# Two graph attention layers on one core: both layers as one program over one arena, the second layer's first loads issued during the last head of the first

## The chip, the cores and the metric

The kernel runs on one core of a Trainium2 chip. The core has five engines with instruction streams of their own: TensorE (matmul), VectorE, ScalarE (ACT), GpSimd (POOL) and SyncE (SP), which here issues all DMA transfers. They meet only through semaphores. The metric is the device time of one execution in microseconds; lower is better.

## The reference

N = 4096 nodes with 256 features, an adjacency matrix of 4096 x 4096 integers. Two layers of masked attention, each followed by a residual addition and a layer norm:

```python
def _gat(x, adj, W_heads, a1, a2, W_out, b_out):            # layer 0: 8 heads of 128
    Wh = jnp.einsum('nf,hfd->hnd', x, W_heads)
    s1 = jnp.einsum('hnd,hd->hn', Wh, a1)
    s2 = jnp.einsum('hnd,hd->hn', Wh, a2)
    e = s1[:, :, None] + s2[:, None, :]
    e = jnp.where(e > 0, e, ALPHA * e)                      # ALPHA = 0.2
    e = jnp.where(adj[None, :, :] > 0, e, NEG)              # NEG = -9e15
    att = jax.nn.softmax(e, axis=-1)
    hp = jax.nn.elu(jnp.einsum('hnm,hmd->hnd', att, Wh))
    feat = jnp.transpose(hp, (1, 0, 2)).reshape(N, NHEADS * NHID)
    return feat @ W_out + b_out
...
x = _layernorm(x + _L0_gnn_ref(x, adj, ...), axis=-1)
x = _layernorm(x + _L1_gnn_ref(x, L1_gnn_W, L1_gnn_a, adj), axis=-1)   # 4 heads of 64, same masked attention, no elu
```

## The kernel before, in words

The attention weights are never computed one by one. With e = s1 + s2, the exponential of the leaky ReLU is one of two products: exp(s1) exp(s2) where e > 0, and the same with the slope 0.2 elsewhere. So for each head and each block of rows the kernel makes two 0/1 patterns (e > 0, and not, each masked by the adjacency) in fp8 and multiplies them with scaled copies of the head's projected features ("u" and "v", each as a high and a low fp16 part), with a column for the sum of the weights.

**Layer 0** (`first_layer`) packs the adjacency into bytes, projects x for all heads, and then runs 64 groups, g = 0 to 63: head g // 8, row block g % 8 of 512 rows. A group is a sweep over 8 column chunks. For each chunk ACT compares (L512), VectorE splits the result into the two patterns (L655, L656), and TensorE multiplies (L426, 256 matmuls in a group) into four output tiles of 128 rows. After the last chunk ACT and VectorE take the sums from PSUM (L530, L661), VectorE divides (`divide`, L669 to L687), ACT takes the exponential for the elu (L518), VectorE adds it (`add_exponentials`, L691), and SP stores the block to the tensor feat in HBM (`store`, L293). The exponential and the addition of group g - 1 come after the first pattern of group g; for group 63 nothing follows. GpSimd makes the next head's operands (`make`) while TensorE sweeps this head; head 7's are its last work in this layer. The pattern buffers are four deep.

**Layer 1** (`second_layer`) begins with a projection stage of 32 row tiles t: load a tile of feat (`load_feat`, 128 rows, all 1024 columns), turn it with 8 transposes (L964), copy it out of PSUM in two halves (ACT L1071, VectorE L1190), multiply by W_out (L974), add x and bias, normalise (`normalise`, L1199 to L1208, with a square root on ACT, L1086), turn the result (L983), compute its scores (L989, L992). VectorE's `weights` (L1216, L1217) makes the columns that the scores multiply by. Then come the operands of 4 heads and 16 sweeps over 1024 rows each (L1023).

The order is written out by hand in each engine's stream; there is no scheduler. Each layer is a block: all five engines meet at its end (L114) and branch into the next. Layer 0 ends when SP has seen its last store land (`sp.wait_ge(s_st, 16 * G)`), and each layer allocates its own buffers. Layer 1's weights are therefore loaded at the start of its block, and TensorE's stream there begins with:

```python
            turn(0)
            pe.wait_ge(s_w, 96)
            for t in range(NT):
                if t + 1 < NT:
                    turn(t + 1)
                if t == 2:
                    pe.wait_ge(s_wa, 1)
                if t > 1:
                    scores(t - 2)
                project(t)
                if t > 0:
                    turn_x1(t - 1)
```

## Time and profile before

| | |
|---|---|
| median of 3 runs | 2853.63 us (2853.56 to 2857.46) |
| the profiled execution | 2853.23 us, its span 2851.1 us |
| TensorE matmuls busy | 2715.6 us, 95% of the span |
| weight loads | 2350.4 us, 82% |
| ACT | 2049.5 us, 72% |
| VectorE | 1964.6 us, 69% |
| GpSimd | 571.5 us, 20% |

The page of the profile cuts the span into 40 slices and gives each engine's busy share in tenths. The lines of TensorE, of its clock and of the DMA engines:

```profile
PE   7889999999999999999999999999979959999997
PEclk9999999999999999999999999999989989999999
DMA  7985521101010100110111111000054253233330
```

Layer 0 fills the first 29 slices, the projection stage of layer 1 the next three, the operands of its heads the 33rd, its sweeps the rest. TensorE is full in nearly all of them; less full are the start, the passage between the layers, the operand stage, and the end.

### The profile page before, as it was taken

The numbers are of one execution on the slowest core, as the hardware profiler recorded it, in microseconds if no ns is written. First come the engines' busy times: TensorE is split into PE (matmuls) and PEld (weight loads), VectorE is DVE, ScalarE is ACT, GpSimd is POOL, SyncE is SP. The second block draws the span as 40 slices with busy tenths as digits, with TensorE's granted clock in tenths as the row PEclk, the third lists the DMA queues.
The fourth block names the chain that finished last, engine by engine and source line by source line (L and its number), as shares of the span: only waits on it lengthen the run. The fifth ranks groups of instructions, "written<-read, shape, count | busy, mean of one in ns | idle before, by whom it ended". The sixth has DMA issues, their size and how long they took to land. (4 is left out here: it accounts for less than half of the span.)

```text
span 2851.1 us, 62563 instructions
## 1 busy us (share of the span) xinstructions
PE 2715.6 (95%) x26702; PEld 2350.4 (82%) x26702; DVE 1964.6 (69%) x3079; ACT 2049.5 (72%) x3213; POOL 571.5 (20%) x447
## 2 busy tenths in 40 slices
PE   7889999999999999999999999999979959999997
PEld 3448887888888888888888888888868849999997
DVE  5456678777677776776776777755544468889887
ACT  4457876878787878777777777777612279999996
POOL 0130026323232322321432323300011150000000
PEclk9999999999999999999999999999989989999999
DMA  7985521101010100110111111000054253233330
GB/s 257 398 302 174 168 88 40 34 25 40 22 36 19 42 28 26 36 33 25 37 29 30 36 30 29 23 21 23 13 168 143 95 188 105 86 106 106 110 110 16
DMA packets 189144, 235.19 MB, mean 82 GB/s; under 512 B 13594, under 2 KB 113050, under 8 KB 188860
## 3 DMA queue, kind: packets, MB, share of 16 engines
q1 hardware_dynamic: 188868, 231.20, 25.2%
q8 instruction: 211, 3.46, 0.5%
q14 instruction: 65, 0.53, 0.1%
HBM read 180.49 MB, written 50.66 MB: 81 GB/s over the span
## 5 line engine op out<-in xcount | busy, mean ns | idle before, releaser
L426 PE MATMUL l_ps<-l_uv,l_bc 128*128 128x258 f16 x16384 | 1835.1, 273 | 7.2 <-POOL l_uv L246 3.4
L426 PEld LDWEIGHTS l_ps<-l_uv,l_bc 128*128 128x128 fp8e4 x16384 | 1592.4, 97 | 247.7 <-DVE l_bc L656 4.8
L512 ACT ACTIVATE l_bc<-l_s1b,l_kc 128x512 fp8e4<-128x512 f32 x2048 | 1281.3, 708 | 89.3 <-PE l_ps L426 89.2
L655 DVE SCALAR_TENSOR_TENSOR l_bc<-l_bc,mask_t 128x512 uint32<-128x512 uint32 x512 | 468.3, 915 | 410.4 <-ACT l_bc L512 408.0
L1023 PE MATMUL l_ps<-l_uv,l_bc 128*128 128x130 f16 x8192 | 489.2, 221 | 44.7 <-DVE l_bc L1297 41.2
L1023 PEld LDWEIGHTS l_ps<-l_uv,l_bc 128*128 128x128 fp8e4 x8192 | 484.2, 98 | 49.9 <-DVE l_bc L1297 48.4
L656 DVE TENSOR_TENSOR l_bc<-l_bc,mask_t 128x512 uint32<-128x512 uint32 x512 | 489.1, 955 | 0.0
L1116 ACT ACTIVATE l_bc<-l_s1b,l_kc 128x1024 fp8e4<-128x1024 f32 x432 | 453.5, 1140 | 0.7 <-PE l_ps L1023 0.5
L239 POOL TENSOR_TENSOR l_tu<-l_whx,l_eu 128x516 f32<-128x516 f32 x56 | 63.7, 1138 | 1172.9 <-PE l_ps L426 1171.1
L530 ACT COPY l_e<-l_ps 128x258 f32<-128x258 f32 x256 | 93.5, 368 | 245.2 <-PE l_ps L426 245.2
L661 DVE SCALAR_TENSOR_TENSOR l_e<-l_ps,l_sc,l_e 128x258 f32<-128x258 f32 x256 | 116.8, 480 | 148.0 <-ACT l_e L530 148.0
L1296 DVE SCALAR_TENSOR_TENSOR l_bc<-l_bc,mask_t 128x1024 uint32<-128x1024 uint32 x128 | 157.1, 1227 | 32.3 <-ACT l_bc L1116 30.9
L1297 DVE TENSOR_TENSOR l_bc<-l_bc,mask_t 128x1024 uint32<-128x1024 uint32 x128 | 156.6, 1224 | 0.0
L393 PE MATMUL l_ps<-mask_t 128*128 128x512 f32 x264 | 129.0, 628 | 0.0
L974 PE MATMUL l_ps<-l_uv 128*128 128x256 f32 x512 | 119.4, 386 | 0.3 <-issue 0.3
L518 ACT ACTIVATE l_e<-l_e 128x512 f32<-128x512 f32 x64 | 40.6, 635 | 109.7 <-DVE l_e L687 109.7
L239 POOL TENSOR_TENSOR l_tv<-l_whx,l_ev 128x516 f32<-128x516 f32 x64 | 93.0, 1453 | 89.4 <-DMA l_whx<-l_wh 88.5
L974 PEld LDWEIGHTS l_ps<-l_uv 128*128 128x128 f32 x512 | 95.2, 191 | 18.7 <-issue 7.0
L246 POOL TENSOR_TENSOR l_uv<-l_tv,l_uv 128x516 f16<-128x516 f32 x64 | 97.1, 1518 | 28.0 <-DVE l_uv L642 28.0
L240 POOL TENSOR_TENSOR l_uv<-l_whx,l_ev 128x516 f16<-128x516 f32 x64 | 93.3, 1458 | 0.0
L617 DVE TENSOR_SCALAR l_uv<-l_uv 128x1024 fp8e4<-128x1024 int32 x52 | 40.3, 775 | 74.3 <-ACT l_uv L496 74.3
L1082 ACT COPY l_bc<-l_ps 128x256 f32<-128x256 f32 x32 | 11.9, 372 | 107.6 <-PE l_ps L983 107.6
(156 smaller groups left out, 1461.8 us busy)
## 6 DMA issues: line engine op xcount, KB each, us to landing
l_uv<-in_adj SPq DMA_DIRECT2D x128, 512.0 KB, 7.1
l_uv<-uv SPq DMA_DIRECT2D x128, 260.0 KB, 5.2
l_s1b<-l_srow SPq DMA_DIRECT2D x64, 256.0 KB, 3.3
l_whx<-l_wh SPq DMA_DIRECT2D x64, 256.0 KB, 4.5
feat<-l_e SPq DMA_DIRECT2D x64, 256.0 KB, 2.4
l_uv<-feat SPq DMA_DIRECT2D x32, 512.0 KB, 3.8
l_wh<-l_bc SPq DMA_DIRECT2D x38, 256.0 KB, 9.2
uv<-l_uv SPq DMA_DIRECT2D x8, 1040.0 KB, 4.7
```

The costliest lines, as they stand in the source:

```text
L239: nc.gpsimd.tensor_tensor(t[:, :, :], whx[k][:, :, :], factor(f, h, c), ALU.mult)
L393: last = nc.tensor.matmul(banks[i % 3], rowsof, wall[:, k, q * H // 2:(q + 1) * H // 2, :], start=(k == 0), stop=(k == KF - 1))
L426: last = nc.tensor.matmul(sums(t, m), pattern(k, m).bitcast(F8)[:, j, t * P:(t + 1) * P], uv[:, slot(h, order[k]) + j, 2 * m * W1:2 * (m + ...
L512: ins = act.activation(pattern(k, 0).bitcast(F8)[:, j, :], s1b[q][:, :], ACT.Relu, bias=kc[:, h, jt:jt + 1], scale=STEEP, saturate=False)
L655: dve.scalar_tensor_tensor(c, v, ONE8X4, m, ALU.bitwise_xor, ALU.bitwise_and)
L656: dve.tensor_tensor(v, v, m, ALU.bitwise_and).then_inc(s_bc, 1)
L661: dve.scalar_tensor_tensor(e1[:, t, :], sums(t, 1), sc[:, g // NB, at:at + 1], e1[:, t, :], ALU.mult, ALU.add).then_inc(s_ev, 1)
L974: last = nc.tensor.matmul(py[t % 2], ft[t % 2][:, k, :], wo[:, k, :], start=(k == 0), stop=(k == KO - 1))
L1023: last = nc.tensor.matmul(sums(t, m), pattern(k, m).bitcast(F8)[:, j, t * P:(t + 1) * P], uv[:, q, at:at + 2 * W1], start=(k == 0 and j == ...
L1116: ins = act.activation(pattern(k, 0).bitcast(F8)[:, j, :], s1b[:, q, :], ACT.Relu, bias=kc[:, g % H, jt:jt + 1], scale=STEEP, saturate=False)
L1296: dve.scalar_tensor_tensor(c, v, ONE8X4, m, ALU.bitwise_xor, ALU.bitwise_and)
L1297: dve.tensor_tensor(v, v, m, ALU.bitwise_and).then_inc(s_bc, 1)
```

## The change

One function, `network`, and one block take the place of the two. The buffers of both layers are views of one array, `arena`, at byte offsets written out by hand; layer 1's views overlap those of layer 0, and semaphores order the reuse. The identity matrix, which lay in a buffer that layer 0 later overwrites, gets a tensor of its own, and layer 1 uses the same one.

- SP: `load_next` issues layer 1's weights and the first four tiles of x in group 57 (g == LAST + 1), after waiting for head 7's operands and for the end of head 6's sweeps. Feature tiles 0 to 2 are issued in group 60, tile 3 in group 63 after three chunks. `load_feat` waits for the store of the row block that it reads. The store of group 63 is issued in the projection stage at t = 1.
- TensorE: the transposes of feature tiles 0 and 1 follow the last sweep; waits for single evacuations protect the PSUM banks.
- VectorE: `weights` is cut in two and runs inside groups 60 and 61; its reduction for the largest weight moves to t = 4. The division of group 63 comes after the copies of feature tiles 0 and 1, its addition after the normalisation of tile 0.
- ACT: the exponential of group 63 comes after the copies of tiles 0 and 1. The activation at the start of layer 1 that loaded the square root's table is gone.
- GpSimd: adds the bias to the first four x tiles when they land.

The diff, cut to its core (functions of layer 1 that are only renamed, with a 2 at their end, are left out):

```diff
-def first_layer(nc, mask_t, x, adj, W, a1, a2, feat):
+def network(nc, x, adj, W, a1, a2, feat, W_out, b_out, Wn, c1, c2, x1, out):
...
+        mask_t = s.sb("mask", [P, NT, N], U8)
+        arena = s.sb("arena", [P, 96208], U8)
+        ident_t = s.sb("ident", [P, P], F32)
+        ident = ident_t[:, :]
...
+        uv = at(0, F16, 2, (CPB + TWIN) * JC, 4 * W1)
+        bc = at(53664, U8, 1, nbuf, 2, JC * blk)
...
+        z = at(75168, F32, 4, TPB2, F)
+        e2 = at(83360, F32, 4, TPB2, 2 * V1)
+        wall2 = at(87552, F32, 4, KF2, HD2 + 2 * H2)
...
+        wo = low_half[:, 0:2 * K].rearrange("p (k f) -> p k f", k=KO)
+        fin = [low_half[:, (2 + u) * K:(3 + u) * K] for u in range(4)]
+        ft = [low_half[:, (6 + p) * K:(7 + p) * K].rearrange("p (k c) -> p k c", k=KO) for p in range(2)]
...
+            pool.wait_ge(s_w, 96)
+            for t in range(NT):
+                pool.wait_ge(s_xl2[t % 4], 16 * (t // 4 + 1))
+                nc.gpsimd.tensor_tensor(xin[t % 4], xin[t % 4], bb, ALU.add).then_inc(s_xb, 1)
+                if t == 4:
+                    nc.gpsimd.memset(units2, 1.0).then_inc(s_un, 1)
...
+            def load_feat(t):
+                sp.wait_ge(s_st, 16 * (LAST + t // TPB + 1))
+                sp.dma_start(fin[t % 4], feat[t * P:(t + 1) * P, :]).then_inc(s_fl[t % 4], 16)
...
+            def load_next():
+                sp.wait_ge(s_uv, H * CPB)
+                sp.wait_ge(s_pe, HC * (H - 1))
+                sp.dma_start(wo, W_out.rearrange("(k p) f -> p k f", p=P)).then_inc(s_w, 16)
+                sp.dma_start(bb, b_out.unsqueeze(0).to_broadcast([P, F])).then_inc(s_w, 16)
+                for m, a in enumerate((c1, c2)):
+                    sp.dma_start(abc2[:, m, :].rearrange("p (h e) -> p h e", h=H2),
+                                 a.unsqueeze(0).to_broadcast([P, H2, D2])).then_inc(s_w, 16)
+                for k in range(KF2):
+                    sp.dma_start(wall2[:, k, 0:HD2].rearrange("p (h e) -> p h e", h=H2),
+                                 Wn[:, k * P:(k + 1) * P, :].rearrange("h p e -> p h e")).then_inc(s_w, 16)
+                for t in range(4):
+                    load_x2(t)
 
...
-            store(G - 1)
-            sp.wait_ge(s_st, 16 * G)
+                if g == LAST + 1:
+                    load_next()
+                if g == LAST + 4:
+                    for t in range(3):
+                        load_feat(t)
+            sp.wait_ge(s_pe, CPB * (G - 1) + 3)
+            load_feat(3)
+            for t in range(NT):
+                if t + 4 < NT:
+                    sp.wait_ge(s_tp2, t + 1)
+                    load_feat(t + 4)
+                if t == 1:
+                    store(G - 1)
+                if t > 0:
+                    sp.wait_ge(s_z, t)
+                    if t + 3 < NT:
+                        load_x2(t + 3)
+                    sp.wait_ge(s_x1, t)
+                    sp.dma_start(x1[(t - 1) * P:t * P, :], x1s[(t - 1) % 4]).then_inc(s_xs[(t - 1) % 4], 16)
...
+            def turn2(t):
+                pe.wait_ge(s_fl[t % 4], 16 * (t // 4 + 1))
+                if t < 2:
+                    pe.wait_ge(s_ev, TPB * (G - 1) + t + 1)
+                if t > 1:
+                    pe.wait_ge(s_ta, t - 1)
+                    pe.wait_ge(s_td, t - 1)
+                for k in range(KO):
+                    last = nc.tensor.transpose(pt[t % 2][2 * k // KO][:, k % (KO // 2), :],
+                                               fin[t % 4][:, k * P:(k + 1) * P], ident)
+                last.then_inc(s_tp2, 1)
...
+            def project2(t):
+                pe.wait_ge(s_ta, t + 1)
+                pe.wait_ge(s_td, t + 1)
+                if t > 1:
+                    pe.wait_ge(s_z, t - 1)
+                else:
+                    pe.wait_ge(s_ev, TPB * (G - 1) + 3)
+                for k in range(KO):
...
+            turn2(0)
+            pe.wait_ge(s_w, 96)
+            for t in range(NT):
+                if t + 1 < NT:
+                    turn2(t + 1)
+                if t == 2:
+                    pe.wait_ge(s_wa2, 2)
+                if t > 1:
+                    scores2(t - 2)
+                project2(t)
+                if t > 0:
+                    turn_x1(t - 1)
...
-            exponentials(G - 1)
+            copy_feat(0)
+            for t in range(NT):
+                if t + 1 < NT:
+                    copy_feat(t + 1)
+                if t > 1:
+                    copy_scores(t - 2)
+                if t > 0:
+                    copy_x1(t - 1)
+                if t == 0:
+                    exponentials(G - 1)
+                root(t)
+            copy_scores(NT - 2)
...
+            def weights2(m):
+                dve.wait_ge(s_w, 96)
+                ch = Chain(dve, s_ch2, 4 * m)
+                for k in range(KF2):
+                    ch.link(dve.tensor_tensor(prod2, wall2[:, k, 0:HD2], abc2[:, m, :], ALU.mult))
+                    ch.link(dve.tensor_reduce(wall2[:, k, HD2 + m * H2:HD2 + (m + 1) * H2],
+                                              prod2.rearrange("p (h e) -> p h e", h=H2), AX.X, ALU.add))
+                dve.sem_inc(s_wa2, 1)
+
+            def weights_peak():
+                dve.tensor_reduce(peaks2[:, H2:H2 + 1], wall2[:, :, 0:HD2], AX.XY, ALU.max, apply_absolute_value=True)
...
+                    if m == 3 and LAST + 4 <= g < LAST + 6:
+                        weights2(g - LAST - 4)
...
-                divide(g)
-            add_exponentials(G - 1)
...
+                if g < G - 1:
+                    divide(g)
             copy_feat(0)
             for t in range(NT):
                 if t + 1 < NT:
...
+                if t == 0:
+                    divide(G - 1)
                 normalise(t)
                 if t == 0:
-                    dve.wait_ge(s_w, 96)
-                    weights()
-            factors()
```

VectorE around the end of layer 0, before: the end of the division, the addition, the meeting, and layer 1's first copies.

```order
L685 TENSOR_TENSOR l_e<-l_e,l_zr 128x4x128
L687 TENSOR_SCALAR l_e<-l_e 128x4x128
L691 SCALAR_TENSOR_TENSOR l_e<-l_e 128x4x128
L114 UNCONDITIONAL_BRANCH
L1182 UNCONDITIONAL_BRANCH
L1184 MEMSET l_warm 128x1
L1190 COPY l_uv<-l_ps 128x512 x2
L1199 TENSOR_TENSOR l_z<-l_ps,l_z 128x256
```

And now, from the last evacuations (L1119) on. Every buffer is a part of the arena, so the lines tell more than the names: L1155 copies feature tiles, L1127 to L1145 are the division, L1164 begins the normalisation.

```order
L1119 SCALAR_TENSOR_TENSOR l_arena<-l_ps,l_arena 128x258 x4
L1155 COPY l_arena<-l_ps 128x512 x2
L1127 TENSOR_TENSOR l_arena<-l_arena 128x4x129
L1131 TENSOR_SCALAR l_arena<-l_arena 128x4
L1133 TENSOR_TENSOR l_arena<-l_arena 128x4
L1135 SCALAR_TENSOR_TENSOR l_arena<-l_arena 128x128
L1141 RECIPROCAL l_arena<-l_arena 128x4
L1135 SCALAR_TENSOR_TENSOR l_arena<-l_arena 128x128 x3
L1143 TENSOR_TENSOR l_arena<-l_arena 128x4x128
L1145 TENSOR_SCALAR l_arena<-l_arena 128x4x128
L1164 TENSOR_TENSOR l_arena<-l_ps,l_arena 128x256
```

The two copies moved ahead of the whole division; the addition (L1149) now stands behind the six instructions of the first normalisation.

SP before, from the last loads and stores of layer 0 into layer 1:

```order
L279 DMA l_s1b<-l_srow 128x512
L293 DMA feat<-l_e 128x4x128
L284 DMA l_mnb<-mean 128x128
L293 DMA feat<-l_e 128x4x128 x2
L114 UNCONDITIONAL_BRANCH
L861 UNCONDITIONAL_BRANCH
L864 DMA l_uv<-feat 128x1024
L883 DMA l_uv<-in_L_gnn_W_out 128x8x256
L884 DMA l_e<-in_L_gnn_b_out 128x256
L864 DMA l_uv<-feat 128x1024
L867 DMA l_z<-in_x 128x256
L888 DMA l_s1b<-in_L_gnn_a 128x4x64 x2
```

And now, in groups 57 and 58 (L414 is a row load, L428 a store, L419 a load of the mean):

```order
L414 DMA l_arena<-l_srow 128x512
L428 DMA feat<-l_arena 128x4x128
L419 DMA l_arena<-mean 128x128
L453 DMA l_arena<-in_L_gnn_W_out 128x8x256
L454 DMA l_arena<-in_L_gnn_b_out 128x256
L456 DMA l_arena<-in_L_gnn_a 128x4x64 x2
L459 DMA l_arena<-in_L_gnn_W 128x4x64 x2
L435 DMA l_arena<-in_x 128x256 x4
L414 DMA l_arena<-l_srow 128x512
L428 DMA feat<-l_arena 128x4x128
```

The loads of the weights and of x moved from behind the meeting to between the stores of groups 56 and 57.

## Rows read from the trace of the kernel before

**Rows 1.** Busy us (x instructions) by stretch; at the end clock, DMA share, GB/s

```profile
500.00:700.00 200.00, 200.00 (x1793) 173.99 (x1792) 142.35 (x217) 152.68 (x260) 58.94 (x42) 1.00 0.10 27
...
1900.00:2060.00 160.00, 160.00 (x1435) 139.22 (x1433) 86.02 (x166) 120.43 (x204) 0.00 (x0) 1.00 0.07 20
...
2066.00:2077.40 11.40, 0.00 (x0) 0.02 (x1) 4.50 (x13) 2.12 (x3) 0.63 (x3) 0.60 0.27 90
2077.40:2085.90 8.50, 1.94 (x8) 1.55 (x8) 0.69 (x1) 0.58 (x1) 0.00 (x0) 0.50 1.07 301
...
2099.40:2110.00 10.60, 10.56 (x64) 9.37 (x64) 5.61 (x18) 2.51 (x10) 1.45 (x2) 1.00 0.43 150
```

**Rows 2.** Timeline of TensorE at the passage: start, duration, what [idle before]

```profile
2054.75 10.77 PE L426 MATMUL l_ps<-l_uv,l_bc 128*128 128x258 f16 x95
2077.41 1.94 PE L964 MATMUL l_ps<-l_ident,l_uv 128*128 128x128 f32 x8 [11.89 <-DMA l_uv<-feat]
2085.95 1.97 PE L964 MATMUL l_ps<-l_ident,l_uv 128*128 128x128 f32 x8 [6.59 <-DMA l_wall<-in_L_gnn_W]
2087.71 4.16 PE L974 MATMUL l_ps<-l_uv 128*128 128x256 f32 x16
...
2099.44 3.69 PE L974 MATMUL l_ps<-l_uv 128*128 128x256 f32 x16 [0.28 <-issue]
...
2103.19 1.04 PE L964 MATMUL l_ps<-l_ident,l_uv 128*128 128x128 f32 x8
2104.06 0.51 PE L989 MATMUL l_ps<-l_wall,l_bc 128*128 128x8 f32 x4
...
2105.03 3.72 PE L974 MATMUL l_ps<-l_uv 128*128 128x256 f32 x16
2108.59 0.38 PE L983 MATMUL l_ps<-l_ident,l_z 128*128 128x128 f32 x2
```

**Rows 3.** Timeline of VectorE and ACT between the last sweep and layer 1

```profile
2066.02 0.48 DVE L661 SCALAR_TENSOR_TENSOR l_e<-l_ps,l_sc,l_e 128x258 f32<-128x258 f32 x1 [1.30 <-ACT l_e L530]
...
2069.97 0.63 ACT L518 ACTIVATE l_e<-l_e 128x512 f32<-128x512 f32 x1 [3.98 <-DVE l_e L687]
2070.64 0.69 DVE L691 SCALAR_TENSOR_TENSOR l_e<-l_e 128x512 f32<-128x512 f32 x1 [0.70 <-ACT l_e L518]
2074.06 1.28 ACT L1065 ACT_TABLE_LOAD   x1 [3.46 <-PEq L114]
```

**Rows 4.** DMA issues from 2040 to 2100: count, KB each, median us to landing

```profile
l_wall<-in_L_gnn_W SPq DMA_DIRECT2D x2, 128.0 KB, 7.2
```

**Rows 5.** Timeline of VectorE and ACT in the first tiles of the projection

```profile
2094.07 0.42 DVE L1216 TENSOR_TENSOR l_s1b<-l_wall,l_s1b 128x256 f32<-128x256 f32 x1
...
2097.49 0.42 DVE L1217 TENSOR_REDUCE l_wall<-l_s1b 128x4 f32<-128x256 f32 x1
...
2098.66 0.68 DVE L1190 COPY l_uv<-l_ps 128x512 f32<-128x512 f32 x1
...
2103.24 0.42 DVE L1199 TENSOR_TENSOR l_z<-l_ps,l_z 128x256 f32<-128x256 f32 x1 [1.22 <-PE l_ps L974]
...
2104.57 0.20 ACT L1086 ACTIVATE l_rt<-l_rt 128x1 f32<-128x1 f32 x1 [0.81 <-DVE l_rt L1204]
...
2105.00 0.41 DVE L1208 TENSOR_SCALAR l_z<-l_z,l_mv,l_rs 128x256 f32<-128x256 f32 x1
```

**Rows 6.** Timeline of ACT at layer 1's exponentials, behind a copy ending at 2272.11

```profile
2272.12 1.28 ACT L1147 ACT_TABLE_LOAD   x1
```

**Rows 7.** Timeline of GpSimd in group 56: its last instruction in layer 0

```profile
1850.97 1.58 POOL L246 TENSOR_TENSOR l_uv<-l_tv,l_uv 128x516 f16<-128x516 f32 x1
```

**Rows 8.** Timeline of VectorE in group 61: a split

```profile
1994.65 0.69 DVE L655 SCALAR_TENSOR_TENSOR l_bc<-l_bc,mask_t 128x512 uint32<-128x512 uint32 x1 [1.15 <-ACT l_bc L512]
```

**Rows 9.** Costliest groups: count, busy us, mean ns, idle before, releaser

```profile
L426 PE MATMUL l_ps<-l_uv,l_bc 128*128 128x258 f16 x16384 | 1835.1, 273 | 7.2 <-POOL l_uv L246 3.4
...
L512 ACT ACTIVATE l_bc<-l_s1b,l_kc 128x512 fp8e4<-128x512 f32 x2048 | 1281.3, 708 | 89.3 <-PE l_ps L426 89.2
```

More of the change, by code:

```diff
@@ L355, in _ @@
+            for p in range(2):
+                sp.wait_ge(s_fin[p], 1)
+                sp.dma_start(tiles(out, NB2 - 1)[:, p * TPB2 // 2:(p + 1) * TPB2 // 2, :],
+                             z[:, p * TPB2 // 2:(p + 1) * TPB2 // 2, :]).then_inc(s_o, 16)
+            sp.wait_ge(s_o, 16 * (NB2 + 1))
         @block.tensor
@@ new lines, in rows_pair @@
+            def rows_pair(u):
+                if u >= 8:
+                    pe.wait_ge(s_tu, u - 7)
+                elif u == 6:
+                    pe.wait_ge(s_f2, 1)
+                elif u == 7:
+                    pe.wait_ge(s_sc, NT)
+                for j in range(2):
+                    for k in range(KF2):
+                        last = nc.tensor.matmul(ps2[:, u % 8, j * HD2:(j + 1) * HD2], xt2[:, 2 * u + j, k, :],
+                                                wall2[:, k, 0:HD2], start=(k == 0), stop=(k == KF2 - 1))
+                last.then_inc(s_pw2, 1)
@@ new lines, in final_stats, with final_norm @@
+            def final_stats(b, tiles):
+                dve.wait_ge(s_dz, H2 * (b + 1))
+                for u in tiles:
+                    last = dve.bn_stats(st[:, u, :], z[:, u, :])
+                last.then_inc(s_n, 1)
+            def final_norm(b):
+                at = 2 * NT + 2 * b
+                dve.wait_ge(s_n, at + 1)
+                ch = Chain(dve, s_n, at + 1)
+                for u in range(TPB2):
+                    last = dve.bn_aggr(mv[:, u, :], st[:, u, :])
+                ch.link(last)
+                dve.tensor_scalar(rt[:, :], mv[:, :, 1:2].rearrange("p u a -> p (u a)"), LN_EPS, None,
+                                  ALU.add).then_inc(s_sd, 1)
@@ L1361, in _ @@
                 if u > 0:
-                    low(u - 1)
+                    low2(u - 1)
                 if u == PAIRS - 3:
-                    split(0, 0)
-            low(PAIRS - 1)
-            compare(0, 1)
-            split(0, 1)
-            for g in range(G):
-                turns = [(g, k) for k in range(ahead, CPB)] + ([(g + 1, k) for k in range(ahead)] if g + 1 < G else [])
+                    split2(0, 0)
+            low2(PAIRS - 1)
+            compare2(0, 1)
+            split2(0, 1)
@@ L1370, in _ @@
+            for g in range(G2):
+                turns = [(g, k) for k in range(ahead2, CPB)] + ([(g + 1, k) for k in range(ahead2)] if g + 1 < G2 else [])
                 if g == 0:
-                    compare(0, ahead)
+                    compare2(0, ahead2)
                 for m, (gk, k) in enumerate(turns):
                     if m + 1 < len(turns):
-                        compare(*turns[m + 1])
-                    elif g + 1 < G:
-                        compare(g + 1, ahead)
-                    split(gk, k)
```

1054 lines of the change are left out of this document (465 added, 589 removed).

## The prediction, on record before the changed kernel ran

> **What bounds the kernel now.** I read the table by stretch first [rows 1]: in the 160 us before 2060 TensorE is busy all the time, and between 500 and 700 us likewise, at a granted clock of 1.00. The attention sweeps of layer 0 are bound by TensorE's own pitch, 1793 matmuls in 200 us, 111.5 ns each, 28.5 us for the 256 of a group; what ACT, VectorE, GpSimd and the queues do there costs nothing as long as they stay ahead. Then the table shows a hole: from 2066.0 to 2077.4 TensorE does nothing, from 2077.4 to 2085.9 it works 1.94 of 8.5 us while the DMA engines are saturated (1.07, 301 GB/s), and from 2099.4 on it is full again.
>
> The timeline of TensorE [rows 2] says what is in the hole. The last sweep matmul ends at 2054.75 + 10.77 = 2065.52. The next instruction, the transposes of feature tile 0 (L964), starts at 2077.41 after 11.89 us idle, released by the load of that tile. The transposes of tile 1 start at 2085.95 after 6.59 us idle, released by the last weight load; the product of tile 0 (L974) follows at 2087.71, that of tile 2 at 2099.44, that of tile 3 at 2105.03. From product 2 on, tiles follow every 5.6 us with TensorE full [rows 1].
>
> VectorE and ACT [rows 3] explain the 11.89 us: after the sweep come the last evacuation (ends 2066.50), the division (until the exponential starts at 2069.97: 3.4 us), the exponential, the last addition (ends 2071.33), and the store of the block, which has to land. At 2074.06, 2.73 us later, the engines start the next program together. Only then does SP issue loads, all at once, and the weights among them take 7.2 us from issue to landing [rows 4].
>
> **The change, part by part.**
>
> The join. Removed are the store's landing, the meeting, the waits for the first loads, the wait for the weight products, and the cold clock. I follow the new stream of TensorE from the sweep's end with the durations and pitches of before. At full clock eight transposes take 1.04 us and the next instruction starts 0.87 after them (2103.19 to 2104.06); a product takes 3.72 and is followed after 3.56 (2105.03 to 2108.59); the scores add 0.97 (2104.06 to 2105.03) and the transposes of x1 the remaining 0.2 of the 5.6 [rows 2]. Consecutive instructions overlap by some 0.1 us, so the transposes of tile 0 start at about 2065.45 and end at 2066.5; they use the PSUM banks of output tile 0, evacuated long before. Transposes of tile 1 start at 2066.3. The product of tile 0 needs both copies of tile 0: VectorE leaves the evacuation at 2066.50, its copy takes 0.68 [rows 5], so 2067.2, plus 0.1 to release: 2067.3. Transposes 2 start at 2070.9, product 1 at 2071.75, the transposes of x1 tile 0 at 2075.3, transposes 3 at 2075.5, scores 0 at 2076.4, product 2 at 2077.4. Before, it was 2099.44. **The saving is 22.0 us**, and behind product 2 both kernels run the same stream at the same pitch. In parts: 11.9 and 6.6 us of idle time, 1.3 from product 2 starting 5.6 instead of 6.9 us behind its predecessor, and 2.2 of slow clock.
>
> Does VectorE supply this? Between the copy of tile 1 (2067.4 to 2068.1) and the copy of tile 2 it now holds the division of group 63 (3.4 us [rows 3]), the normalisation of tile 0, and the addition (0.69). The division ends at 2071.5; product 0 has ended at 2071.0, so the normalisation starts at once, and its value for the root is ready 1.3 us later (2103.24 to 2104.57 [rows 5]), at 2072.9. ACT's exponential runs from 2071.6 to 2072.2; then its table of functions must be switched for the square root, 1.28 us [rows 6], to 2073.5. The root ends at 2073.7 and x1 of tile 0 stands 0.64 later (2104.77 to 2105.41 [rows 5]), at 2074.4. TensorE asks for it at 2075.3: 0.9 us in hand. The addition ends at 2075.05, the copy of tile 2 at 2075.8, wanted at 2077.4: 1.6 in hand. The normalisation of tile 1 waits for product 1 at 2075.5 and takes its usual course. So I cost the moved division and addition at nothing; products 0 and 1, 7.4 us of TensorE, hide them, and beyond the 0.9 us in hand each us would cost one.
>
> On the table switch, the trace shows 1.28 us, begun 0.01 us after the copy before it (2272.12 [rows 6]). The Trainium skill, page "ScalarE: Activation LUTs", section "What ACT_TABLE_LOAD costs", counts a drain of 1.38 us on top, 2.66 in all. With the row x1 of tile 0 is 0.9 us early; by the page it would come at 2075.8, 0.4 us late, and the sum would be 21.6 instead of 22.0. I go by the row.
>
> The loads moved into head 7. SP issues ten (W_out, the bias, two of a, two of W, four tiles of x) in group 57, behind the store of group 56. They wait for head 7's operands, which GpSimd finished at 1852.55 [rows 7], and for head 6's sweeps; group 57 begins 7 times 28.6 us before 2065.5, at 1865.3. So neither wait holds. Queued behind them on SP are the row load of group 59 and the store of group 57, both wanted only a sweep later; even at the 7.2 us landing of the crowded case [rows 4] the ten are over within a sweep. Three feature tiles follow at group 60, the fourth in group 63 once three column chunks are done, at about 2048, to be used at 2075.5. DMA was busy 0.07 there [rows 1]. Cost: nothing. Without this cover it is the old 6.6 us.
>
> The weight products. Eight VectorE instructions leave the projection and come as twice four into the sweeps of groups 60 and 61. All eight took 2094.07 to 2097.91, so 1.9 us for four [rows 5]. Between two splits VectorE sits idle 1.15 us, waiting for ACT [rows 8], and ACT itself waits for TensorE to free a pattern buffer, 89.3 us over the run [rows 9]: the patterns are made as early as the buffers allow. One split is thus 0.8 us late and the next one on time. Nothing; uncovered it would be 3.8.
>
> GpSimd adds the bias to four tiles in head 7, where it was idle from 1852.55 [rows 7]; by the 0.42 us that VectorE takes for the same form [rows 5] to twice that, at most 3.4 us in which splits could be stretched, inside the same slack. The peak over the weights moves to tile 4, where VectorE works about half of the 5.6 us. SP's store of group 63 now stands ahead of x tile 4, wanted some 15 us later. Nothing for each.
>
> What the trace of before does not show is how the engines behave with no pause, and with the buffers placed anew. Below: more than 22.0 would need faster sweeps, which full TensorE at a fixed pitch excludes, or a tighter overlap of the first copies than I place; I allow 1 us, 23.0. Above: if the first transposes and product 0 ran at the slow clock in spite of no idle time, they would take 0.9, 0.9 and 0.4 us more (1.94, 1.97 and 4.16 against 1.04, 1.04 and 3.72 [rows 2]), saving 19.8; if the chain of tile 0 came 3 us later than I place it, 19.9 at full clock; both at once 17.7. I take full clock, since the rows nearest to the case, TensorE full before and behind the hole, show it.
>
> **From the saving to the time.** The profiled execution's 2853.23 us become 2831.2. It lies 0.4 us below the median of the runs (2853.63), so I name 2831.6.
>
> **Rivals.**
>
> *The join is bound by VectorE and ACT.* The division and the exponential, moved behind the first transposes, take the place of the load wait: TensorE waits at the transposes of x1 tile 0, or at the scores. For it: only 0.9 us is in hand over a chain of a dozen handovers. Against it: each link has its duration in rows 3, 5 and 6. A delay of 2 to 6 us beyond the slack gives 2833 to 2838. Chance 0.12.
>
> *The loads are not early after all.* If the weights were still late at the join, 6.6 us stay: 2838. SP would have to be held in group 57 past 2060, and GpSimd's last operand stands at 1852.55. Chance 0.02.
>
> *Slower: the sweeps lose pitch.* All operands now lie in one buffer at other offsets, and the sweeps of layer 0 are 16384 matmuls [rows 9] at 111.5 ns, 1827 us without slack. Each 1% they lose costs 18.3 us; from 1.2% on the saving is gone. At 2% it is 36.5 us: 2868. For it: nothing absorbs a change there. Against it: 1793 matmuls per 200 us with GpSimd writing (500 to 700) and 1435 per 160 without it are one and the same pitch [rows 1], so the engine does not answer to its neighbours. Chance 0.03.
>
> *Nothing gained*, because what follows is held by something else. That would be a queue or VectorE setting the 5.6 us of a tile, but TensorE is full there [rows 1], so all later tiles shift. Within 0.2% of 2853.6: chance 0.02.
>
> **How the numbers follow.** The forecast has 0.81, with a range of its own of 2830.0 to 2833.5; the rivals as above. The range reaches up over most of the first rival and the bound of 17.7 us, to 2836.5, and down to 23 us saved and the scatter of the runs, 2829.5. A measurement of this kernel can tell about 0.2%, 5.7 us, from no change. Faster takes the forecast, the first rival and the late loads, 0.95; same 0.02; slower 0.03.
>
> **What would show it.** Right: the transposes of tile 0 follow the last sweep matmul within 0.2 us and take 1.04; the granted clock is 1.00 over the join; product 2 starts 12 us after the sweep's end (33.9 before); 5.6 us a tile; sweeps at 1793 per 200 us; the ten loads at about 1872. Wrong: idle time before the transposes of x1 tile 0 or the scores of tile 0, released by VectorE or ACT (first rival), or by a load (second); fewer matmuls per 200 us (third).

## The result and the profile after

The changed kernel takes 2831.69 us (median of 6 runs, 2830.11 to 2834.51), the one before, beside it, 2855.57 (2853.56 to 2857.46). The ratio is 0.9917, with a 95% interval of 0.9905 to 0.9930. The profiled execution took 2831.95 us, with a span of 2830.2 against 2851.1 before. The forecast was 2831.6. The medians lie 23.9 us apart, and the interval of the ratio makes that 20.0 to 27.1 us.

The busy table by stretch of the profile after, same columns as [rows 1], has no hole any more:

```profile
500.00:700.00 200.00, 200.00 (x1793) 173.97 (x1792) 142.41 (x217) 152.68 (x260) 58.95 (x42) 1.00 0.10 27
...
1900.00:2060.00 160.00, 160.00 (x1435) 139.26 (x1434) 89.90 (x175) 121.10 (x205) 0.00 (x0) 1.00 0.12 33
...
2066.00:2070.00 4.00, 4.00 (x28) 3.60 (x27) 3.06 (x9) 1.55 (x3) 0.00 (x0) 1.00 0.45 148
2070.00:2078.00 8.00, 8.00 (x51) 7.02 (x50) 6.34 (x20) 3.62 (x9) 0.00 (x0) 1.00 0.37 117
2078.00:2100.00 22.00, 22.00 (x135) 19.22 (x135) 9.65 (x28) 4.59 (x21) 3.77 (x6) 1.00 0.53 170
```

TensorE (second column) is busy in all of the 34 us from 2066 on, at a granted clock of 1.00, where the two long pauses of [rows 2] alone were 18.5 us before. The first two rows are the sweeps: 1793 and 1435 matmuls, the same counts as in [rows 1].

The timeline of TensorE after, answering to [rows 2]. L660 is the sweep, L685 the transposes of features, L697 the product, L708 the transposes of x1 (the normalised result of layer 0), L714 the scores. Transposes t, product t and scores t are those of row tile t; the join is the stretch from the last sweep matmul to product 2:

```profile
2051.84 14.35 PE L660 MATMUL l_ps<-l_arena 128*128 128x258 f16 x127
2066.03 1.91 PE L685 MATMUL l_ps<-l_ident,l_arena 128*128 128x128 f32 x16
2067.89 3.69 PE L697 MATMUL l_ps<-l_arena 128*128 128x256 f32 x16
2071.42 1.04 PE L685 MATMUL l_ps<-l_ident,l_arena 128*128 128x128 f32 x8
2072.29 3.62 PE L697 MATMUL l_ps<-l_arena 128*128 128x256 f32 x16
2075.75 0.38 PE L708 MATMUL l_ps<-l_ident,l_arena 128*128 128x128 f32 x2
...
2076.84 0.51 PE L714 MATMUL l_ps<-l_arena 128*128 128x8 f32 x4
...
2077.81 3.72 PE L697 MATMUL l_ps<-l_arena 128*128 128x256 f32 x16
```

No row has a bracket of idle time. The sweep ends at 2051.84 + 14.35 = 2066.19 and product 2 starts at 2077.81, 11.62 us later. Before it was 2099.44 - 2065.52 = 33.92 [rows 2], so the join gained 22.30. The sweep ended 0.67 later in this execution and what follows product 2 took 752.39 us instead of 751.66; both lie inside the scatter between executions (in the ten traces in which product 2 is not slowed, what follows its start takes 751.6 to 753.1 us; the sweep's end is treated in the last section), and 22.30 - 0.67 - 0.73 is the 20.9 between the spans.

VectorE and ACT at the same place after, answering to [rows 3], [rows 5] and [rows 6]: the last evacuation (L1119), the end of the division (L1145), the exponential (L861), the value for the root (L1169), the table switch and the root (L894), x1 of tile 0 (L1173), the copy of tile 2 (L1155):

```profile
2066.69 0.48 DVE L1119 SCALAR_TENSOR_TENSOR l_arena<-l_ps,l_arena 128x258 f32<-128x258 f32 x1 [1.30 <-ACT l_arena L873]
...
2071.54 0.43 DVE L1145 TENSOR_SCALAR l_arena<-l_arena 128x512 f32<-128x512 f32 x1
...
2073.01 0.15 DVE L1169 TENSOR_SCALAR l_arena<-l_arena 128x1 f32<-128x1 f32 x1
...
2074.38 0.41 DVE L1173 TENSOR_SCALAR l_arena<-l_arena 128x256 f32<-128x256 f32 x1
...
2075.31 0.68 DVE L1155 COPY l_arena<-l_ps 128x512 f32<-128x512 f32 x1
...
2072.00 0.64 ACT L861 ACTIVATE l_arena<-l_arena 128x512 f32<-128x512 f32 x1 [3.44 <-DVE l_arena L1145]
2072.65 1.28 ACT L894 ACT_TABLE_LOAD   x1
2073.95 0.20 ACT L894 ACTIVATE l_arena<-l_arena 128x1 f32<-128x1 f32 x1
```

x1 of tile 0 stands at 2074.79, and TensorE comes to it at 2075.75: 0.96 us in hand. The copy of tile 2 ends at 2075.99, wanted at 2077.81: 1.8 in hand.

The queues and GpSimd in head 7, after: the first and the last of SP's ten loads (L453 and, x4, L435), GpSimd's additions of the bias (L377) with the split that VectorE makes beside them (L1113, L1114), and VectorE at the end of the first four weight products (L1181):

```profile
1873.30 0.39 SPq L453 DMA_DIRECT2D l_arena<-in_L_gnn_W_out  x1
...
1880.56 3.77 SPq L435 DMA_DIRECT2D l_arena<-in_x  x4
...
1884.98 2.09 POOL L377 TENSOR_TENSOR l_arena<-l_arena 128x256 f32<-128x256 f32 x3 [31.77 <-DMA l_arena<-in_x]
1886.52 1.10 DVE L1113 SCALAR_TENSOR_TENSOR l_arena<-l_arena,l_mask 128x512 uint32<-128x512 uint32 x1 [1.85 <-ACT l_arena L855]
1887.55 1.21 DVE L1114 TENSOR_TENSOR l_arena<-l_arena,l_mask 128x512 uint32<-128x512 uint32 x1
...
1966.84 0.42 DVE L1181 TENSOR_REDUCE l_arena<-l_arena 128x4 f32<-128x256 f32 x1
1967.41 0.69 DVE L1113 SCALAR_TENSOR_TENSOR l_arena<-l_arena,l_mask 128x512 uint32<-128x512 uint32 x1
...
1969.16 0.69 DVE L1113 SCALAR_TENSOR_TENSOR l_arena<-l_arena,l_mask 128x512 uint32<-128x512 uint32 x1 [0.46 <-ACT l_arena L855]
```

The loads are issued from 1873.30 on. GpSimd uses the x tiles from 1884.98 on, VectorE's weight products use W and a in groups 60 and 61 (the first four end at 1967.26), and TensorE uses W_out from 2067.89 on. The split behind the weight products has no idle time ahead of it, the one after that has 0.46 us again: VectorE was late for one split and on time for the next.

### The profile page after: what moved, and what is told of

The parts are those of the page before. It is cut to its first block, busy times and chain, and to the rows that moved or that the text cites. A ratio compares the mean times of both kernels' runs of the same rounds, so it can differ in the third digit from the quotient of the medians.

```text
span 2830.2 us, 62581 instructions
## 1 busy us (share of the span) xinstructions
PE 2714.5 (96%) x26702; PEld 2350.6 (83%) x26702; DVE 1964.6 (69%) x3078; ACT 2049.7 (72%) x3212; POOL 571.4 (20%) x445
## 3 DMA queue, kind: packets, MB, share of 16 engines
q8 instruction: 211, 3.46, 0.5%
## 4 chain that ended last, share of the span: by engine, by line
PE 73%; DVE 4%; ACT 4%; POOL 2%; issue 1%; ACTq 0%; DVEq 0%; POOLq 0%
PE l_ps L660 56%; PE l_ps L748 11%; PE l_ps L697 4%; ACT l_arena L924 3%; PE l_ps L685 1%; DVE l_arena L1263 1%; DVE l_arena L1262 1%; PE l_ps L717 1%; DVE l_arena L1270 1%; POOL l_arena L370 1%; ACT l_arena L936 1%; POOL l_arena L357 0%; PE l_ps L714 0%; DVE l_arena L1290 0%; DVE l_arena L1251 0%
## 5 line engine op out<-in xcount | busy, mean ns | idle before, releaser
L660 PE MATMUL l_ps<-l_arena 128*128 128x258 f16 x16384 | 1833.3, 273 | 7.1 <-POOL l_arena L346 3.4
L660 PEld LDWEIGHTS l_ps<-l_arena 128*128 128x128 fp8e4 x16384 | 1591.7, 97 | 246.4 <-DVE l_arena L1114 4.3
L855 ACT ACTIVATE l_arena<-l_arena 128x512 fp8e4<-128x512 f32 x2048 | 1281.4, 708 | 89.3 <-PE l_ps L660 89.2
L1113 DVE SCALAR_TENSOR_TENSOR l_arena<-l_arena,l_mask 128x512 uint32<-128x512 uint32 x512 | 468.9, 916 | 407.3 <-ACT l_arena L855 404.6
L748 PE MATMUL l_ps<-l_arena 128*128 128x130 f16 x8192 | 491.6, 222 | 42.9 <-DVE l_arena L1263 40.9
L748 PEld LDWEIGHTS l_ps<-l_arena 128*128 128x128 fp8e4 x8192 | 486.6, 98 | 48.1 <-DVE l_arena L1263 46.5
L1114 DVE TENSOR_TENSOR l_arena<-l_arena,l_mask 128x512 uint32<-128x512 uint32 x512 | 489.9, 957 | 0.0
L924 ACT ACTIVATE l_arena<-l_arena 128x1024 fp8e4<-128x1024 f32 x432 | 453.4, 1141 | 1.2 <-PE l_ps L748 1.2
L339 POOL TENSOR_TENSOR l_arena<-l_arena 128x516 f32<-128x516 f32 x120 | 156.9, 1307 | 1263.4 <-PE l_ps L660 1170.4
L1119 DVE SCALAR_TENSOR_TENSOR l_arena<-l_ps,l_arena 128x258 f32<-128x258 f32 x256 | 116.9, 481 | 146.4 <-ACT l_arena L873 146.4
L346 POOL TENSOR_TENSOR l_arena<-l_arena 128x516 f16<-128x516 f32 x120 | 176.4, 1489 | 32.1 <-DVE l_arena L1100 27.7
L1262 DVE SCALAR_TENSOR_TENSOR l_arena<-l_arena,l_mask 128x1024 uint32<-128x1024 uint32 x128 | 157.2, 1228 | 33.1 <-ACT l_arena L924 31.6
L340 POOL TENSOR_TENSOR l_arena<-l_arena 128x516 f16<-128x516 f32 x120 | 174.5, 1454 | 0.0
L861 ACT ACTIVATE l_arena<-l_arena 128x512 f32<-128x512 f32 x64 | 40.7, 635 | 109.1 <-DVE l_arena L1145 109.1
L697 PE MATMUL l_ps<-l_arena 128*128 128x256 f32 x512 | 118.9, 385 | 0.0
L697 PEld LDWEIGHTS l_ps<-l_arena 128*128 128x128 f32 x512 | 94.6, 190 | 18.4 <-issue 6.6
L377 POOL TENSOR_TENSOR l_arena<-l_arena 128x256 f32<-128x256 f32 x32 | 23.3, 730 | 348.9 <-DMA l_arena<-in_x 348.9
```

Of the source, the lines that this page charges most:

```text
L339: nc.gpsimd.tensor_tensor(t[:, :, :], whx[k][:, :, :], factor(f, h, c), ALU.mult)
L340: last = nc.gpsimd.tensor_tensor(part(h, c, j), whx[k][:, :, :], factor(f, h, c), ALU.mult)
L346: last = nc.gpsimd.tensor_tensor(part(h, c, j + 1), t[:, :, :], part(h, c, j), ALU.subtract)
L660: last = nc.tensor.matmul(sums(t, m), pattern(k, m).bitcast(F8)[:, j, t * P:(t + 1) * P], uv[:, slot(h, order[k]) + j, 2 * m * W1:2 * (m + ...
L697: last = nc.tensor.matmul(py[t % 2], ft[t % 2][:, k, :], wo[:, k, :], start=(k == 0), stop=(k == KO - 1))
L748: last = nc.tensor.matmul(sums2(t, m), pattern2(k, m).bitcast(F8)[:, j, t * P:(t + 1) * P], uv2[:, q, at:at + 2 * V1], start=(k == 0 and j ...
```

## The experiments

Each kernel is the changed one with a part put back or added, timed beside the kernel before on the same chip, whose median there was 2855.6 to 2856.5 us. Two numbers are read from each: the time, and, in its trace, how long behind the last sweep matmul product 2 starts (33.92 us before, 11.62 after). The second has none of the scatter of the 2050 us ahead of it.

**The changed kernel again.**

> The changed kernel itself, once more, as the reference for the three experiments that share its chip. Both theories expect 2831.7 us within the scatter of 0.1%, a saving of 22 to 24 us, TensorE without idle time from the last sweep matmul to the product of tile 2, and that product 11.6 us behind the sweep's end.

2832.31 us (2830.67 to 2833.54), ratio 0.9920 [0.9905, 0.9934]. Product 2 again starts 11.62 us behind the sweep, though the sweep ends 1.2 us later (2067.42) and the rest takes 752.75. So in these two traces the join repeats to the hundredth, and their scatter lies outside it.

**Both undone, the one block of memory kept.** The store of the last block, its landing, the division, the exponentials and the addition all stand ahead of layer 1 again; the loads and the weight products follow them.

```diff
-                if g == LAST + 1:
-                    load_next()
-                if g == LAST + 4:
-                    for t in range(3):
-                        load_feat(t)
-            sp.wait_ge(s_pe, CPB * (G - 1) + 3)
-            load_feat(3)
+            store(G - 1)
+            sp.wait_ge(s_st, 16 * G)
+            load_feat(0)
...
+            pe.wait_ge(s_st, 16 * G)
```

> Still one block and one arena, but the order of the kernel before at the join: division, exponential and addition first, SP waits for the last store to land and only then issues layer 1's first loads, the weight products stand behind the first normalisation. My theory (only order and waits count; placement of buffers, the missing branch and the single block are worth nothing): product 2 at 33 to 34 us behind the sweep's end, 2853 to 2856 us, the same as the kernel before within 0.1%. Rival (a part of the gain comes from the arena or from having one block): 2 us or more faster than before.

2855.31 us (10 runs, 2851.22 to 2859.34), ratio 0.9998 [0.9989, 1.0007]. TensorE's timeline:

```profile
2059.80 6.08 PE L668 MATMUL l_ps<-l_arena 128*128 128x258 f16 x53
2077.31 1.94 PE L693 MATMUL l_ps<-l_ident,l_arena 128*128 128x128 f32 x8 [11.43 <-issue]
2085.93 1.97 PE L693 MATMUL l_ps<-l_ident,l_arena 128*128 128x128 f32 x8 [6.69 <-DMA l_arena<-in_L_gnn_W]
2087.70 5.65 PE L705 MATMUL l_ps<-l_arena 128*128 128x256 f32 x16
...
2100.69 3.72 PE L705 MATMUL l_ps<-l_arena 128*128 128x256 f32 x16
```

Product 2 starts at 2100.69, the sweep ends at 2065.88, so 34.8 us; 33 to 34 were expected. Both long waits are back (11.43 and 6.69 us for 11.89 and 6.59), and the excess over the 33.9 of before is mostly product 0, which takes 5.65 us for 4.16. To about 0.1% of the time the new placing of all buffers is worth nothing in either direction, and the whole gain lies in what this kernel undoes.

**Only the meeting kept.** Loads and weight products stay in head 7.

> Loads stay early, but the end of layer 0 is put back in front of layer 1: division, exponential and addition of the last group come first on VectorE and ACT, SP stores and waits for the landing, and TensorE's first transposes wait for it. My theory: addition ends 5.8 us after the sweep's end, the store lands 2.3 us later, so the transposes start 8.3 us after the sweep's end; TensorE restarts at the slow clock, which costs about 2 us more until product 2: product 2 at 22 us after the sweep's end, 2831.7 + 10.5 = 2842.2 us. Rival (loads early are the whole gain, since the engines' tail work has to be done anyhow): 2833 us.

2843.00 us (2840.20 to 2843.98), ratio 0.9956 [0.9941, 0.9971]. TensorE's timeline around the join in this kernel:

```profile
2059.82 6.30 PE L660 MATMUL l_ps<-l_arena 128*128 128x258 f16 x55
2074.23 3.68 PE L685 MATMUL l_ps<-l_ident,l_arena 128*128 128x128 f32 x16 [8.11 <-DMA feat<-l_arena]
...
2087.87 3.72 PE L697 MATMUL l_ps<-l_arena 128*128 128x256 f32 x16
```

Here the wait is the landing of the stored block, 8.11 us; the 16 transposes behind it take 3.68 us instead of 1.91. Product 2 starts 21.75 us behind the sweep; 22 was expected.

**Only the loads put back to the join** (and the weight products with them, which need the weights).

> Only the early issue of the loads is undone: layer 1's weights, the x tiles and the feature tiles are issued when the last sweep has ended, in the order of the kernel before, and the weight products go back behind the first normalisation. There is still no meeting of the engines and the last store is waited for by nobody. My theory (two separate waits in series, each worth its own time): SP issues from the sweep's end on; the weights then took 11.9 us from the first issue to landing in the kernel before (2074.07 to 2085.95), so TensorE's second set of transposes starts about 12 us after the sweep's end, product 2 about 13.5 us later, 25.4 us after the sweep's end against 11.6: 2831.7 + 13.8 = 2845.5 us. Rival (the meeting and the landing of the store are the whole cost, the loads would be hidden behind the division and the exponential): product 2 at 15 us after the sweep's end, 2835 us.

2850.18 us (10 runs, 2846.52 to 2852.89), ratio 0.9980 [0.9971, 0.9989]. Its timeline of TensorE:

```profile
2070.78 1.97 PE L694 MATMUL l_ps<-l_ident,l_arena 128*128 128x128 f32 x8 [3.44 <-DMA l_arena<-feat]
2079.38 1.97 PE L694 MATMUL l_ps<-l_ident,l_arena 128*128 128x128 f32 x8 [6.63 <-DMA l_arena<-in_L_gnn_W]
2081.14 5.06 PE L706 MATMUL l_ps<-l_arena 128*128 128x256 f32 x16
...
2094.00 0.78 PE L723 MATMUL l_ps<-l_arena 128*128 128x8 f32 x4 [2.37 <-DVEq L1192]
...
2095.65 4.72 PE L706 MATMUL l_ps<-l_arena 128*128 128x256 f32 x16
```

The transposes of tile 1 start 12.03 us behind the sweep, as expected (12), but product 2 only at 28.3 instead of 25.4. The weight products, placed behind the moved normalisation and addition, hold the scores for 2.37 us, and two products run slowed (5.06 and 4.72 us for 3.72). That is a miss of 4.7 us in the time, 2.9 of it at the join. It cuts against a simple sum of two separate parts: undoing one half alone costs more, and doing one half alone brings less. Against 34.8 us with both undone, early loads alone bring 13.1 and no meeting alone 6.5, together 19.6; both bring 23.2. Of the 3.6 left over some 2 us are the slow clock: either half alone leaves a long wait, with slowed instructions behind it. Another 1.5 are the wait on the weight products, 0.85 us with both undone and 2.37 with the loads alone at the join.

**The division alone ahead of the first copies.**

```diff
+            divide(G - 1)
             copy_feat(0)
...
-                if t == 0:
-                    divide(G - 1)
```

> One line moved: on VectorE the division of the last group stands in front of the copy of feature tile 0 instead of behind the copy of tile 1. My theory: the copy of tile 0 ends at 0.5 + 3.4 + 0.7 = 4.6 us after the sweep's end, product 0 starts 4.9 to 5.2 instead of 1.7 us after it, TensorE idles about 3.3 us in front of it, and nothing later gives it back: 2831.7 + 3.4 = 2835.1 us. Rival (the join has slack, so the order on VectorE does not matter): 2831.7 us.

2836.54 us (2833.75 to 2838.36), ratio 0.9933 [0.9916, 0.9949]. Timeline of TensorE, and the busy table of the pause and of the product behind it (columns as in the first table; the third from the end is the granted clock):

```profile
2072.39 5.37 PE L697 MATMUL l_ps<-l_arena 128*128 128x256 f32 x16 [3.37 <-issue]
```

```profile
2069.00:2072.30 3.30, 0.02 (x1) 0.00 (x0) 3.17 (x11) 1.16 (x2) 0.00 (x0) 1.00 0.84 286
2072.30:2077.60 5.30, 5.21 (x17) 4.33 (x18) 0.59 (x1) 1.34 (x2) 0.00 (x0) 0.68 0.05 20
```

Product 0 starts 5.12 us behind the sweep (4.9 to 5.2 expected). The bracket names no releaser, but on VectorE the copy of tile 0 now starts at 2071.60, behind the end of the division, and takes 0.69 us, to 2072.29, 0.1 us ahead of product 0. The 3.4 us of the division are the idle time, so products 0 and 1 do hide it in the changed kernel. But the product behind the pause takes 5.37 us, 1.65 more than at full clock, with 0.68 granted on average. Product 2 starts at 2083.99, 16.7 us behind the sweep, not 15.0.

**The weight products alone back at the join.**

```diff
-                    if m == 3 and LAST + 4 <= g < LAST + 6:
-                        weights2(g - LAST - 4)
...
                     add_exponentials(G - 1)
+                    weights2(0)
+                    weights2(1)
```

> Only the weight products are moved back from the sweeps of groups 60 and 61 to VectorE's stream behind the first normalisation and the last addition; loads stay early. My theory: eight instructions of 0.46 us hold the scores of tile 0 until about 3.8 us after the addition's end, 2.4 us later than now, so TensorE idles 2.4 us in front of the scores and product 2 comes 2.4 us later: 2834.1 us, up to 1.7 us more if the slow clock follows the pause as it did in the divide-first kernel, 2835.8. Rival (the weight products hide behind products 0 and 1): 2831.7 us, no idle time at the scores.

2835.50 us (2833.25 to 2837.76), ratio 0.9929 [0.9914, 0.9944]. The scores wait 2.15 us for VectorE, product 2 is 14.04 us behind the sweep: 2.4 more, inside the 2.4 to 4.1 that follow from the expected times. No slow clock followed the pause in the trace, which is of the fastest of the four runs. They lie in two pairs, 2833.25 and 2833.61, 2837.39 and 2837.76; no trace shows whether the clock fell in the slower pair.

**Four times the weight products, in the sweeps.** Six more pairs of instructions go ahead of each two, so VectorE's piece grows from 1.9 to 7.5 us.

```diff
+                        for _ in range(6):
+                            more.link(dve.tensor_tensor(prod2, wall2[:, 0, 0:HD2], abc2[:, 0, :], ALU.mult))
+                            more.link(dve.tensor_reduce(wall2[:, 0, HD2 + n * H2:HD2 + (n + 1) * H2],
+                                                        prod2.rearrange("p (h e) -> p h e", h=H2), AX.X, ALU.add))
                         weights2(n)
```

> The weight products are made four times in each of groups 60 and 61 (sixteen instructions, 7.5 us in one piece instead of 1.9), to measure the cover of the moved work. My theory: patterns are ready 2.7 us before TensorE takes them up, and VectorE regains 1.15 us per split; 7.5 us in one piece delay the split of the last chunk to about 2.5 us past its use, so TensorE idles about 2.5 us in each of the two groups: 2831.7 + 5 = 2836.7 us. Rival (VectorE's idle time of some 10 us in a group absorbs it wherever it stands): 2831.7 us.

2837.18 us (2834.30 to 2837.41), ratio 0.9931 [0.9915, 0.9948]. TensorE in the sweeps of groups 60 and 61:

```profile
1976.08 28.78 PE L660 MATMUL l_ps<-l_arena 128*128 128x258 f16 x256 [2.21 <-DVE l_arena L1114]
2007.06 8.22 PE L660 MATMUL l_ps<-l_arena 128*128 128x258 f16 x72 [2.20 <-DVE l_arena L1114]
```

The waits are 2.2 us each (2.5 expected), so the sweeps cover 5.3 us of such a piece (the time, 2837.18, agrees with the 2836.7 expected); the 1.9 us of the changed kernel are well inside.

**Three, six and nine more instructions in the chain of x1 tile 0.** They are VectorE multiplications of 0.42 us whose result is not used, between the statistics and the value for the root.

```diff
                 ch.link(dve.bn_aggr(mv[:, u, :], st[:, u, :]))
+                if t == 0:
+                    hold = Chain(dve, s_pad)
+                    for _ in range(9):
+                        hold.link(dve.tensor_tensor(prod2, wall2[:, 0, 0:HD2], abc2[:, 0, :], ALU.mult))
```

> Nine dependent VectorE instructions of 0.46 us (a product into a buffer nobody reads any more) are put into the normalisation of tile 0, ahead of the value for the square root: 4.1 us. My theory: this chain has 1.7 us in hand at that place, 0.75 because the root waits for the table switch anyway and 0.96 until TensorE asks for x1 of tile 0; so TensorE idles 2.4 us at the transposes of x1 tile 0, released by VectorE: 2834.1 us, up to 2835.8 with the slow clock behind it. Rival (VectorE's chain already bounds the join, no slack): 4.1 us, 2835.8 and more.

> Three further VectorE instructions of 0.42 us (0.46 with their handover) stand in the normalisation of x1 tile 0; their result is not used. By nine of them 2.33 us of idle time were left of 4.1 added, so 1.7 to 1.8 us are in hand. Theory: the 1.4 us of three stay inside it, TensorE has no pause at the join, product 2 starts 11.6 us after the sweep, and the time is that of the changed kernel, 2831.7 to 2832.3. Rival (only the 0.96 us read in the trace are in hand): 0.4 us of idle time ahead of the transposes of x1 tile 0, 2832.1 to 2832.7, product 2 at 12.0 or later; the timeline tells them apart, the time cannot.

> Six of the same instructions, 2.75 us added to the chain of x1 tile 0. Theory A: 1.0 to 1.1 us of idle time ahead of the transposes of x1 tile 0 and no slower clock behind it, product 2 at 12.7 us after the sweep, 2832.8. Theory B: any pause at this place lets the granted clock fall behind it, as with nine: the 1.1 us of idle time and 3.3 us of slowed instructions (x1 transposes, transposes 3, scores, product 2), product 2 at 14.5 to 15, 2836.1. Theory C (my prediction's rule, each us beyond 0.9 in hand costs one): 1.8 us idle and no more, product 2 at 13.4, 2833.5.

TensorE with six, and with nine; then the busy table with nine:

```profile
2075.08 0.44 PE L708 MATMUL l_ps<-l_ident,l_arena 128*128 128x128 f32 x2 [0.94 <-DVE l_arena L1177]
...
2077.20 3.72 PE L697 MATMUL l_ps<-l_arena 128*128 128x256 f32 x16
```

```profile
2079.98 0.69 PE L708 MATMUL l_ps<-l_ident,l_arena 128*128 128x128 f32 x2 [2.33 <-DVE l_arena L1177]
...
2083.91 5.05 PE L697 MATMUL l_ps<-l_arena 128*128 128x256 f32 x16
```

```profile
2077.60:2080.00 2.40, 0.07 (x2) 0.02 (x1) 1.99 (x7) 0.68 (x2) 0.00 (x0) 0.96 0.00 0
2080.00:2083.90 3.90, 3.90 (x18) 3.29 (x18) 3.40 (x9) 1.07 (x3) 0.48 (x1) 0.50 0.55 155
2083.90:2088.80 4.90, 4.90 (x18) 4.05 (x17) 0.00 (x0) 0.31 (x2) 1.10 (x3) 0.72 0.76 254
```

- Three: 2831.89 us (2830.51 to 2832.65), ratio 0.9919 [0.9904, 0.9934]. No idle time; product 2 at 11.62. The rival of 0.4 us is refuted.
- Six: 2831.19 us (2830.71 to 2835.24), ratio 0.9922 [0.9905, 0.9939]. 0.94 us idle, full clock behind it, product 2 at 12.79 (theory A said 12.7). Theories B and C are refuted by the timeline of this one execution; the times alone could not do it.
- Nine: 2837.93 us (2837.49 to 2840.08), ratio 0.9939 [0.9924, 0.9954], above the theory's 2834.1 to 2835.8. 2.33 us idle (2.4 expected), but behind it the clock is at its lower level, 0.50. Product 2 starts 4.36 us late and itself loses another 1.33 (its successor comes 4.89 us behind it instead of 3.56): 5.7 us for a pause of 2.3.

By six 2.75 - 0.94 = 1.8 us were in hand, by nine 4.1 - 2.33 = 1.8. The idle time counts only from the end of product 1, though, and its successor otherwise starts 0.16 us before that end (3.46 us behind a start of 3.62). Counted by starts the reserve is therefore between 1.6 and 1.7. The timeline of ACT with nine shows why that is more than the 0.96 read above:

```profile
2073.75 0.64 ACT L861 ACTIVATE l_arena<-l_arena 128x512 f32<-128x512 f32 x1 [3.45 <-DVE l_arena L1145]
2074.40 1.28 ACT L894 ACT_TABLE_LOAD   x1
2079.08 0.20 ACT L894 ACTIVATE l_arena<-l_arena 128x1 f32<-128x1 f32 x1 [3.40 <-DVE l_arena L1173]
```

The table load does not wait for the value of the root; it runs right behind the exponential. In the changed kernel the value is ready at 2073.16 and the load ends at 2073.93. These 0.77 us are a second reserve, for VectorE's part of the chain alone: 0.96 + 0.77 = 1.7.

## Why the prediction was right, step by step

*The sweeps keep their pitch.* Right: 1793 matmuls in 200 us before and after. The slower rival had a cause that could have been real, the new offsets; the kernel with both parts undone excludes it to about 0.1%.

*The join, 22.0 us.* Right, 22.3 measured. Counted from the sweep's end, product 0 starts 1.70 us behind it (1.8 predicted), transposes 2 5.23 (5.4), scores 10.65 (10.9), product 2 11.62 (11.9). Of the 0.3 us between 11.9 and 11.6, 0.1 is the earlier start of product 0, another 0.1 is product 1, whose successor came 3.46 us behind it where I had laid 3.56 end to end, and the rest is rounding. That no clock is lost was the right choice between the bounds of 17.7 and 23: the transposes of tiles 0 and 1 take 1.91 us for 16, not twice 1.9.

*VectorE supplies it.* Right, and this was the closest step: 0.9 us in hand predicted, 0.96 measured, though twelve handovers lie in between. On the table switch I had weighed the Trainium skill, page "ScalarE: Activation LUTs", section "What ACT_TABLE_LOAD costs", whose drain of 1.38 us would by the prediction's estimate have made the sum 21.6. The trace does not agree with it here: the load starts 0.01 us behind the exponential and takes 1.28, and the root starts 0.02 behind the load. The measurement decides.

*"Beyond the 0.9 us in hand each us would cost one."* Wrong, and in both directions. For VectorE's part the reserve is 1.7 us, since I had the table load in the chain but not the room beside it. The prediction's own figures held it: the value for the root ready at 2072.9, the table loaded at 2073.5. And beyond the reserve 0.94 us of pause cost 1.2, but 2.33 cost 5.7, since the clock fell. This sentence priced the first rival (2833 to 2838 for 2 to 6 us of delay). Had it come about, that would have been too cheap: a delay of 2.3 us beyond the reserve alone measured 2837.9, where the rule gives 2833.9. The same rule stands in the bound of 19.9 us saved (a chain 3 us late costs 2.1), which was too generous by the same reasoning. The forecast of 22.0 itself did not hang on it, because TensorE never paused.

*The loads in head 7 cost nothing.* Right: issued from 1873.30 on (about 1872 predicted), more than 190 us ahead of TensorE's first use. Without this cover the wait is 6.63 us again, as named.

*The weight products cost nothing.* Right: one split late, the next on time. Uncovered I had put them at 3.8; alone at the join they cost 2.4, since in the changed kernel the addition ends at 2075.40, 1.4 us before TensorE comes to the scores of tile 0.

*GpSimd and SP.* Right: the additions take 2.93 us for four (2.09 + 0.84; bound 3.4). While they run, one split takes 1.10 and 1.21 us instead of 0.69 each; that they are the cause fits the times but was not tested. VectorE's idle time takes it up: the split behind it again waits 1.33 us for ACT.

*From span to time.* That the median came within 0.1 us is luck. The forecast started from the 2853.63 us of three runs, but the kernel before took 2855.57 beside the changed one, 1.9 more. Between the medians 23.9 us were saved, between the profiled spans 20.9, and 22.3 at the join; 22.0 was forecast. The 1.4 us between 20.9 and 22.3 are scatter outside the join. The interval of 20.0 to 27.1 us holds both the 22.0 and the 22.3, so the join, and not the time, is what bears the prediction out.

## What to carry to other kernels

Where the bounding engine runs at a fixed pitch, a hole between two stages can be costed to some tenths of a us by laying the durations of the later, full stage end to end and asking, for each input, when it stands and when it is asked for. Price what would come behind the reserve with the clock in it: at this join pauses of 0.94 and 2.15 us cost 0.2 to 0.3 us more than themselves, those of 2.33 to 3.37 us 1.7 to 3.4 more, each read from one trace. A join with two causes of delay has to be rid of both: either alone brought 13.1 and 6.5 of 23.2 us, the rest came only with the two together.
